# First attention of a two-layer kernel: row maxima spread over all steps, one PSUM block for values and sums, and the diagonal mask of the maxima added by VectorE

## The reference, cut to what matters

```python
A1 = jnp.einsum('bhqd,bhkd->bhqk', Q1, K1) * scaling      # and A2 from Q2, K2
A1 = jnp.where(causal, A1, neg_inf)                       # and A2
attn = jax.nn.softmax(A1, -1) - lam * jax.nn.softmax(A2, -1)
O = jnp.einsum('bhqk,bhkd->bhqd', attn, V)
```

## Time and profile before

| what | value |
| --- | --- |
| median of 3 runs | 4366.25 us (4363.6 to 4369.36) |
| the profiled execution's own time | 4362.48 us |
| its span, first to last instruction | 4360.6 us |
| mean granted TensorE clock | 0.911 |
| PE busy in the span | 3700.6 us (85%) |
| DVE, ACT, POOL busy in the span | 2467.0, 1754.4, 1706.6 us |
| heads 1 to 29, first exponential to first exponential | 420.82 to 2520.39 us |

### The profile page before, as it was taken

One profiled execution on the slowest core, in us unless ns is written; L12 is line 12 of the kernel. 1 busy time (PEld: TensorE's weight loads), 2 busy tenths in 40 slices (PEclk: granted clock), 3 DMA queues, 4 the chain that ended last, 5 costly groups with the idle time before them and its releaser, 6 DMA issues. The chain is left out here.

```text
span 4360.6 us, 69689 instructions
## 1 busy us (share of the span) xinstructions
PE 3700.6 (85%) x21166; PEld 1647.8 (38%) x21231; DVE 2467.0 (57%) x4628; ACT 1754.4 (40%) x3522; POOL 1706.6 (39%) x1117
## 2 busy tenths in 40 slices
PE   6869999999999999999999996753899678896794
PEld 3322333232323232323233323642455445555462
DVE  4456766575757576767676753767211276666102
ACT  2324665666656566666666663110122141111110
POOL 1313555555555555555555554400344231110203
PEclk9978999999999999999999997855899899996897
DMA  4431111111111111111111103210443200001332
GB/s 156 154 120 33 34 37 33 34 35 35 35 35 35 35 35 35 35 36 34 38 33 38 31 9 96 82 40 0 121 91 76 45 24 4 0 0 39 111 111 87
DMA packets 202326, 224.92 MB, mean 52 GB/s; under 512 B 86673, under 2 KB 162706, under 8 KB 195858
## 3 DMA queue, kind: packets, MB, share of 16 engines
q1 hardware_dynamic: 186642, 195.39, 15.3%
q0 software_dynamic: 15360, 25.44, 3.1%
HBM read 139.12 MB, written 80.87 MB: 50 GB/s over the span
## 5 line engine op out<-in xcount | busy, mean ns | idle before, releaser
L638 POOL TENSOR_TENSOR attention_probs<-attention_probs 128x1024 f32<-128x1024 f32 (+2 forms) x640 | 1228.1, 1921 | 1160.2 <-PE attention_ps_o L791 1160.1
L708 DVE TENSOR_REDUCE attention_chunk_max<-attention_ps_m 128x1 f32<-128x512 f32 (+3 forms) x2560 | 1394.2, 604 | 457.4 <-PE attention_ps_m L823 280.6
L683 ACT ACTIVATE attention_probs<-attention_ps_s 128x512 f32<-128x512 f32 (+3 forms) x2560 | 1199.5, 532 | 826.9 <-PE attention_ps_s L772 459.7
L768 PE MATMUL attention_ps_s<-attention_q_stack,attention_k_stack 99*128 99x512 bf16 (+3 forms) x2560 | 821.6, 354 | 91.1 <-ACT attention_probs L683 70.1
L820 PE MATMUL attention_ps_m<-attention_k_stack,attention_q_stack 96*128 96x512 bf16 (+3 forms) x2560 | 772.5, 357 | 48.7 <-DMA attention_v_head<-v_rows 34.5
L791 PE MATMUL attention_ps_o<-attention_probs,attention_v_head 128*32 128x512 f32 (+3 forms) x5120 | 647.4, 558 | 8.6 <-issue 5.0
L768 PEld LDWEIGHTS attention_ps_s<-attention_q_stack,attention_k_stack 99*128 99x128 bf16 x2560 | 234.0, 98 | 668.4 <-ACT attention_probs L683 466.0
L820 PEld LDWEIGHTS attention_ps_m<-attention_k_stack,attention_q_stack 96*128 96x128 bf16 x2560 | 224.9, 97 | 628.7 <-DVE attention_chunk_max L708 490.2
L809 PE MATMUL attention_ps_l<-attention_probs,consts 128*32 128x512 f32 (+1 forms) x2560 | 352.6, 580 | 9.7 <-POOL attention_probs L638 1.0
L734 DVE TENSOR_TENSOR attention_out_sb<-attention_even_sb,attention_odd_sb 64x512 f32<-64x512 f32 x128 | 115.0, 898 | 296.8 <-ACT attention_even_sb L656 290.9
L823 PE MATMUL attention_ps_m<-mask_q_bf,ident_bf 128*128 128x128 bf16 x1024 | 225.5, 223 | 0.0
(11 more groups left out here) (283 smaller groups left out, 4108.8 us busy)
## 6 DMA issues: line engine op xcount, KB each, us to landing
qk_parts<-project_parts SPq DMA_DIRECT2D x64, 384.0 KB, 3.0
heads_out<-attention_out_sb SPq DMA_DIRECT2D x128, 128.0 KB, 2.3
out_heads<-heads_out SPq DMA_DIRECT2D x8, 2048.0 KB, 8.2
experts_w<-in_f_w SPq DMA_DIRECT2D x16, 1024.0 KB, 8.3
attention_q_stack<-qk_parts SPq DMA_DIRECT2D x32, 384.0 KB
attention_k_stack<-qk_parts SPq DMA_DIRECT2D x32, 384.0 KB
experts_w<-in_e_w SPq DMA_DIRECT2D x24, 512.0 KB, 4.8
v_rows<-project_v SPq DMA_DIRECT2D x8, 1024.0 KB, 4.2
```

What stands on the lines that cost most here:

```text
L638: pool.tensor_tensor(probs[:, to, :, lo:], probs[:, to, :, lo:], probs[:, k % RING_P, :, lo:], ALU.add).then_inc(pair_ok, 1)
L683: act.activation(probs[:, k % RING_P, a, left(k):], ps_s[(2 * k + a) % RING_S][:, left(k):], ACT.Exp, scale=float(DH) ** -0.5).then_inc(pr ...
L708: last = dve.tensor_reduce(chunk_max[:, a, jq, c:c + 1], ps_m[m % RING_M][:, 0:width(m)], AX.X, ALU.max)
L768: last = pe.matmul(psum[:, lo:], ks[at][0:WITH_MAX, a, kb * P:(kb + 1) * P], qs[at][0:WITH_MAX, a, tq * GROUP + lo:(tq + 1) * GROUP], star ...
```

## The change

- The maxima are spread. `maxima_at` now gives 42 of the 80 maxima tiles of head n + 2 to steps 20 to 39 of head n (`BEGIN_MAX`), and the other 38 to steps 0 to 17 of head n + 1 (`END_MAX`). The turning stands at k = 18. Head 0 has all 80 of head 1 in its steps 0 to 17, and then 42 of head 2.
- PE's order in an iteration changes. Two thirds of the maxima stand between the scores ahead of the values; values of both steps and the ones of the pair before follow each other in one block.
- In `values` and `ones` the four strips are now two halves of the 512 queries (blocks 0 and 2, blocks 1 and 3) times two a. Each step has its own matmuls of 256 columns, and `ones` runs once in two steps. Values and sums of a turn share one PSUM bank, of which there are two in turn. The matmuls that cleared PSUM, the strips' two halves and their addition on DVE go.
- ACT takes a turn out in one copy of 128x512 (`take`), 3.5 steps after the turn's end (at k = 7, 15, 27 of the head and 3 of the next), after the slot's store has landed.
- A turn is stored in 4 DMAs on one semaphore (`stored`), two for the values and two for the sums, in place of 2 DMAs on two semaphores. The store of turn 2 moves behind the 3 small DMAs.
- The mask matmul of the diagonal maxima goes. DVE adds `mask_wide` and takes the maximum in one `tensor_tensor_reduce`, which writes the masked tile back to PSUM.
- The output stage reads 2 rows of sums per head in place of 4.

The diff, cut to what the text below speaks of:

```diff
+BEGIN_MAX, END_MAX = 20, 18
...
+        def maxima_at(head, k, after, later):
+            early, steps_early = len(MAXIMA) * (N_STEPS - BEGIN_MAX) // (N_STEPS - BEGIN_MAX + END_MAX), N_STEPS - BEGIN_MAX
+            if k >= BEGIN_MAX:
+                n = k - BEGIN_MAX
+                return later, range(n * early // steps_early, (n + 1) * early // steps_early)
+            start = 0 if is_first(head) else early
+            n, rest = min(k, END_MAX), len(MAXIMA) - start
+            return after, range(start + n * rest // END_MAX, start + min(k + 1, END_MAX) * rest // END_MAX)
...
-                for turn in range(Q_TILES):
+                for turn in range(Q_TILES - 1):
                     if head is not None and not (is_first(head.n) and turn == 0):
                         store(head.n, turn)
...
+                if head is not None:
+                    store(head.n, Q_TILES - 1)
...
+                wait_apart(sp, taken, head * Q_TILES + turn + RING_O, core.passed)
+                for half in range(2):
+                    rows = slice(half * 2 * DV, (half + 1) * 2 * DV)
+                    sp.dma_start(oT[...][half], results[rows, slot, 0]).then_inc(stored[slot], 16)
+                    sp.dma_start(sums[...][half],
+                        results[half * 2 * DV:(half + 1) * 2 * DV:DV, slot, 1]).then_inc(stored[slot], 16)
...
+            def take(head, turn):
+                slot = turn % RING_O
+                    act.wait_ge(stored[slot], (head * (Q_TILES // RING_O) + turn // RING_O + 1) * (STORES * 16))
+                act.wait_ge(values_ok, head * N_STEPS + LAST[turn] + 1)
+                act.wait_ge(ones_ok, head * PAIRS + (LAST[turn] + 1) // PAIR + RING_P // PAIR)
+                act.activation(results[:, slot], ps_o[slot][:], ACT.Copy).then_inc(taken, 1)
...
                     for a in range(2):
+                        ended = ends(k, 4)
+                        if a == 1 and ended and not (ended[1] and is_first(head)):
+                            take(head - 1 if ended[1] else head, ended[0])
...
+                    if c == jq // GT:
+                        wait_apart(dve, max_ok, after * N_MAX + m + 1, core.passed)
+                        last = dve.tensor_tensor_reduce(ps_m[m % RING_M][:, 0:w], ps_m[m % RING_M][:, 0:w],
+                                                        mask_wide[:, GROUP - w:], 1.0, -3.0e38, ALU.add, ALU.max, to)
...
+            def strips(k):
+                first = left(k) // P
+                for half in range(2):
+                    block = (first - half + 1) // 2
+                    if block < BLOCKS:
+                        for a in range(2):
+                            yield (half * 2 + a) * DV, half, a, block
...
                     if more:
                         score(head, at, k + 2, 0)
+                        maxima(whose_n, whose_at, items[:third])
                         score(head, at, k + 2, 1)
+                        maxima(whose_n, whose_at, items[third:2 * third])
                         score(head, at, k + 3, 0)
...
                     values(head, at, k)
+                    values(head, at, k + 1)
+                    if k > 0:
+                        ones(head, k // PAIR - 1)
...
+                    if more:
+                        score(head, at, k + 3, 1)
...
+                    maxima(whose_n, whose_at, items[2 * third:])
```

209 lines of the change are left out of this document (73 added, 136 removed).

## The result

| what | before | after |
| --- | --- | --- |
| median (runs) | 4367.01 us (4) | 4510.99 us (4; 4492.46 to 4513.36) |
| ratio to before, 95% interval | | 1.0321 [1.0293, 1.0349] |
| the profiled execution's own time, span | 4362.48, 4360.6 us | 4513.36, 4511.2 us |
| mean granted TensorE clock | 0.911 | 0.894 |
| head 0 | 68.7 us | 88.0 us |

The change made the kernel 3.2% slower. The forecast was 4395 us, with a range of 4275 to 4450, so the direction was right and the size was not.

A forecast was written before the change was run, and what follows sets the result against it. PE was taken to set the pace. The profiled 4362.5 us, plus 32 for heads 1 to 29, less 1 for once-only terms, gave 4393.5; the runs' median lies 3.8 higher, 4397, stated as 4395, range 4275 to 4450.

The forecast's parts named there:

- The store, the term that decides: Turn 1's copy, mid k = 15, waits until 30.8 us for the previous head's turn 3 store; ACT stands 7.1 us.
- The half clock behind it: PE idle during the copy's wait lowers the clock behind it: 1.4 us a head, bounds 0 and 3.
- PE's work: PE's matmul work in a head falls from 64.7 to 59.7 us; an iteration's block off the diagonal takes 1.51.
- rival 5: Half-width passes cost 25 ns each; 36 extra behind k = 15 add 0.9 us a head: 4421 us, chance 0.05.
- The bank waits: An iteration's fourth maxima tile waits for the first's bank: 5.4 us a head, 3.9 behind k = 15.
- The start of a head: The stretch at each head's start, at clock 0.57 before because no maxima fill PE, should be at full clock.
- Rival 1: Bank waits do not come, part behind k = 15 is 3.9 us shorter: 4315 us; full or past turning point, 0.28.
- rivals 1 and 2: The second: the copy finds its store landed, a head takes 65.4 us without clock loss: 4190 us, chance 0.08.
- Rival 4: Masked maximum takes two passes, 1.37 us; banks come late at diagonal tiles, 3 us behind k = 15: 4500, chance 0.07.
- Head 0: Head 0, with all 80 maxima of head 1 in 18 steps, takes 79.5 us in place of 68.7: +11.
- The time ahead of head 0: Maxima ahead of head 0 add 1 us at one pass; first exponential forecast at 353.1 us.

The follow-up runs named there:

- four slots: Changed kernel with four result slots in place of two, one per turn with its own semaphore: 4332.83 us, ratio 0.994.
- Moving the tiles behind the split: Four result slots, and the maxima of the head after next begin in step 22 in place of 20: 4291.0 us, ratio 0.9825.
- the one cast alone: Four result slots, and the rest of the turned maxima kept in PSUM, so DVE's second cast reads PSUM: 4311.23 us, ratio 0.9878.
- Breaking up the four in a row: Four result slots, and two of the four maxima at k = 38 moved behind the ones: 4320.99 us, ratio 0.989.
- The mask on PE: Diagonal maxima masked by PE again, plain DVE reduction: 4490.23 us on the changed kernel; 4199.15 with four result slots and second third of maxima behind ones.
- A shorter reduction: Changed kernel with DVE's plain reductions reading only the first 256 columns of a tile: 4428.78 us, ratio 1.0161.
- the moved third: Second third of an iteration's maxima moved behind the ones: 4433.12 us on the changed kernel; 4214.52 with four result slots.

## Why the prediction was right in direction and wrong in size

- **The store, the term that decides**: right. Copy at 30.7 us for 30.8, ACT's wait 5.7 for 7.1, once in each of 29 heads, shown by four slots (-178 us). ACT's own arrival was about 1.3 us later than forecast. PE's waits for banks ahead of k = 15 were 3.5 us and not 1.6, but that changed nothing while the store was later still.
- **The half clock behind it**: 1.4 us less 0.4 of work in advance was forecast, 1.1 is what four slots took away behind the copy. Right, by the earlier trace rows.
- **PE's work**: right. From the score ahead of a block off the diagonal to what follows it, less 0.22 for the score, 168 undisturbed blocks take 1.53 us; forecast 1.51. All blocks of a head sum to 28.1 us; forecast 27.6. The Trainium skill, TensorEngine Tiling (Array Packing), section Instruction Overhead, would by the prediction's estimate add 25 ns for each of the three extra passes, 1.585 us. The 0.02 us found here are nearer to none, and rival 5 falls.
- **The bank waits: the step that failed.** The prediction had 5.4 us a head, "3.9 of it behind k = 15", from one pattern: a fourth tile 0.88 us behind the first of its own iteration, with DVE idle when the first arrives. Read as distances between starts, less what each matmul takes, PE waits 6.7 us a head ahead of scores and maxima behind k = 15, the copy's wait not counted (6.6 with four slots). So this term was 2.7 us too small. Where the pattern is alone, k = 26 to 38, it is nearly as forecast: 2.6 us in six iterations, 0.44 each. It had left out the places where DVE is not idle or the row of tiles is longer. Around the split of the turned maxima, k = 22 to 24, PE waits 1.9 us. At k = 38 it waits 1.0.
- **What these places cost, by runs.** Moving the tiles behind the split takes 2.0 us net off the part behind the copy, and the one cast alone 0.8. Breaking up the four in a row takes 0.6, of which 0.3 comes back in the next head. The mask on PE, with no 141 ns behind each masked maximum, takes 0.5. A shorter reduction takes 2.3 in all. These prices overlap and are not to be added.
- **A second half clock that the prediction did not have.** The wait behind the turning brought half clock in 10 heads of 29 (none of it in head 9), which take 1.4 us longer there, 0.5 us a head on the mean. With the bank waits that makes 3.2 of the 3.9 us of excess; I can't place the other 0.7. With the moved third and the mask on PE, which both act on these waits, the part is 41.06 us and the excess is gone.
- **The start of a head** was to be at full clock. It is in 21 of 29 heads; the other 8 begin a round of the loop.
- **Rival 1** had the mechanism backwards: the banks came later, not earlier. The price that it put on them, 3.9 us a head, is about what a better order gives back: the part falls from 44.9 to 41.35 with the moved third. The sums of rivals 1 and 2 are wrong: they take 81 and 203 us, which are differences to the kernel before, off the forecast. Off the kernel before (4366) they give about 4284 and 4162, for 4315 and 4190.
- **Rival 4** fell: 701 ns, not 1370. That its 4500 us came close to the measured 4511 is luck. It has the banks late at the diagonal tiles for 3 us behind k = 15, but the mask back on PE gives only 0.5 of it back.
- **Head 0**: +8.5. I added 42.1 us of DVE's time alone to 22 steps at 1.7. The first 18 steps took 45.3 and the other 22 took 42.7, 1.94 each, so most of the miss is in the steps that I took over from before. A shorter reduction gives 79.8 for the head.
- **The time ahead of head 0**: +10.4. The first exponential comes 11.4 us later than before, and the forecast had 1 of it. Of the 11.4, 10.2 are there when the attention's first load is issued (286.53 us for 276.29), so they lie in the projection, whose code is unchanged. The 80 maxima on DVE take 42.7 us for 42.1. PE's clock was 0.92 at 60 to 240 us, before 0.98. In the kernels with the same projection the first exponential came anywhere from 352.1 to 364.1 us (347.7 with the shorter reduction), with no pattern that I see. This stays open.

## What to carry to other kernels

A store that shares a queue with loads and a ring of two slots was harmless here as long as the copy came late; an edit that makes the engines faster, joins two copies or moves them can put it on the path, so ask for each ring which older transfer its next user waits for. When PE runs ahead of DVE over three banks, look at what else stands in DVE's stream at that place: the waits gather where a chain of small operations meets the next tiles, not where the mean rate says, and here a cast of 0.2 us within SBUF stood until POOL's running addition had ended. And work taken off the bound engine is no gain when it lengthens the instruction that frees its banks.

## What the runs showed of the hardware

- `tensor_tensor_reduce` is two instructions on DVE: 701, 565, 426 and 298 ns for 512, 384, 256 and 128 columns, and 141 ns for reading the accumulator each time; the plain reductions take 684, 551, 417 and 283.
- A DVE cast of 32x128 within SBUF stands until POOL's running addition ends: in the changed kernel it began 1.4 to 1.5 us into an addition of 2.35 and ended 0.07 to 0.08 us behind it, in each of the 31 heads that have one; alone, ahead of head 0, it took 0.21 us. In the kernel before, where it began 2.1 to 2.2 us into the addition, it ended 0.07 to 0.08 us behind it as well and took 0.25 to 0.35 us, so the change, which puts it earlier into the addition, made it three times as long. The same cast from PSUM takes 0.28 beside POOL, and so do the subtractions with an operand in PSUM. The Trainium skill, Advanced Engine Details and Errata, section Mode Summary, notes that the second SBUF port of VectorE is shared with GPSIMD, and that GPSIMD instructions and those of VectorE that use both ports block each other. The trace agrees with that, and shows that DVE waited here and that the price (0.63 us) is set by what is left of POOL's instruction and not by the cast.
- The first DMA that follows the seven loads issues for some 20 us whichever store it is: the store of turn 3 for 15.9 to 24.0 us in heads 1 to 29 of the changed kernel, the store of turn 0 for 20.2 to 25.2 us when that one is next. A store with no loads ahead of it issues in 0.65 us. Why the first one is slow, no run shows.
- PE stood for 2.0 to 3.1 us at the start of the 8 heads that begin a round of the loop, and of none of the other 21 of heads 1 to 29 of the changed kernel. Six of these waits have no releaser in the profile.
